# A pairwise interaction kernel with gathered embeddings: longer flights of gathers, seven product slots, a 2 KB descriptor scratch and another order of the work

## What is computed

```python
e = jnp.stack([tbl_0[ids[:, 0]], ..., tbl_31[ids[:, 31]]], axis=1)   # (2048, 32, 64)
row_idx, col_idx = np.triu_indices(32, k=1)
z = jnp.einsum('bpe,fpe,bpf->bp', e[:, row_idx, :], kernel, e[:, col_idx, :])
h = jnp.concatenate([z, dense_ctx], axis=1)
h = jnp.maximum(h @ W_top1 + b_top1, 0.0)
h = jnp.maximum(h @ W_top2 + b_top2, 0.0)
y = h @ W_top3
```

## Time and profile before

| what | us |
|---|---|
| median of 3 runs | 840.17 |
| lowest, highest | 839.22, 840.34 |
| the profiled execution | 839.88 |
| its span, first to last instruction | 838.1 |
| PE, DVE, ACT, POOL busy in the span | 753.0, 651.5, 644.2, 484.0 |
| mean granted clock of PE | 0.976 of full speed |

### The profile page before, as it was taken

How to read it: one execution, slowest core, us unless ns; L and a number is a source line. 1 busy time by engine, 2 the same in 40 slices (tenths; PEclk the granted TensorE clock), 3 DMA queues, 4 the chain that set the end, 5 groups by cost and what they waited for, 6 DMA issues and landing times.

```text
span 838.1 us, 16496 instructions
## 1 busy us (share of the span) xinstructions
PE 753.0 (90%) x4672; PEld 305.5 (36%) x4672; DVE 651.5 (78%) x601; ACT 644.2 (77%) x5196; POOL 484.0 (58%) x518
## 2 busy tenths in 40 slices
PE   0498969889898999999947998999999999999998
PEld 0244545355533333333312233333343333333333
DVE  0388969779677878999946896898978999789950
ACT  0279988967649728899953698799786999999952
POOL 6776776767676776666666766666766666000000
PEclk9999999999999999999979998999999999999999
DMA  9611111211212121111212121121122112000100
GB/s 335 204 40 38 40 38 25 52 25 38 51 27 50 26 51 25 32 42 23 51 24 50 25 48 24 24 50 25 25 50 41 31 24 51 1 2 1 27 1 0
DMA packets 34644, 36.40 MB, mean 43 GB/s; under 512 B 18676, under 2 KB 20980, under 8 KB 34424
## 3 DMA queue, kind: packets, MB, share of 16 engines
q0 software_dynamic: 16384, 16.81, 11.0%
q1 hardware_dynamic: 18168, 18.53, 7.6%
HBM read 26.91 MB, written 0.01 MB: 32 GB/s over the span
## 4 chain that ended last, share of the span: by engine, by line
PE 48%; POOL 31%; issue 11%; DMA 9%; DVE 0%; DVEq 0%; ACT 0%; POOLq 0%
POOL rows L407 21%; PE y_ps L507 15%; PE y_ps L529 11%; POOL kept_rows L407 10%; PE sum_ps L543 9%; DMA rows<-tbl_dram,idx 7%; PE layer_ps L559 3%; DMA kept_rows<-tbl_dram,idx 2%; PE layer_ps L562 2%; PE y_ps L465 1%; PE y_ps L576 1%; PE y_ps L522 1%; PE y_ps L585 1%; PE y_ps L510 1%; PE y_ps L580 0%
## 5 line engine op out<-in xcount | busy, mean ns | idle before, releaser
L669 ACT ACTIVATE batch_products<-batch_products 128x64 f32<-128x64 f32 x2576 | 615.4, 242 | 105.5 <-DVE batch_products L763 105.3
L669 ACT ACTIVATION_READ_ACCUMULATOR batch_products<-batch_products 128x1 f32 x2576 | 486.4, 189 | 0.0
L407 POOL DMA_INDIRECT rows<-tbl_dram,idx x384 | 362.4, 944 | 168.9 <-issue 102.1
L752 DVE TENSOR_TENSOR products<-y_ps,xt 128x1024 f32<-128x1024 f32 (+1 forms) x224 | 255.5, 1197 | 44.2 <-PE y_ps L508 38.5
L763 DVE TENSOR_TENSOR batch_products<-y_ps,kept_rows 128x1024 f32<-128x1024 f32 x192 | 225.1, 1216 | 24.7 <-PE y_ps L531 16.7
L507 PE MATMUL y_ps<-xt,kernel_sb 64*128 64x512 f32 (+1 forms) x448 | 207.8, 598 | 0.4 <-DVE products L752 0.3
L508 PE MATMUL y_ps<-xt,kernel_sb 64*128 64x512 f32 (+1 forms) x448 | 207.8, 598 | 0.0
L529 PE MATMUL y_ps<-kernel_sb,xt 64*128 64x512 f32 x384 | 196.1, 639 | 4.8 <-DVE products L744 2.5
L531 PE MATMUL y_ps<-kernel_sb,xt 64*128 64x512 f32 x384 | 196.1, 639 | 0.0
L543 PE MATMUL sum_ps<-products,selector 128*32 128x512 f32 (+1 forms) x1520 | 155.9, 523 | 4.2 <-ACT z_sb L639 1.7
L407 POOL DMA_INDIRECT kept_rows<-tbl_dram,idx x128 | 120.9, 945 | 57.3 <-issue 35.5
(11 more groups left out here) (54 smaller groups left out, 408.7 us busy)
## 6 DMA issues: line engine op xcount, KB each, us to landing
kernel_sb<-pair_kernel_dram SPq DMA_DIRECT2D x15, 512.0 KB, 11.2
rows<-tbl_dram,idx POOLq DMA_INDIRECT x384, 2.5
special<-xt SPq DMA_DIRECT2D x48, 128.0 KB
kept_rows<-tbl_dram,idx POOLq DMA_INDIRECT x128, 2.5
special<-xt SPq DMA_DIRECT2D x32, 64.0 KB
w_sb<-w_dram SPq DMA_DIRECT2D x1, 1024.0 KB
w_sb<-w_dram SPq DMA_DIRECT2D x1, 512.0 KB
kernel_sb<-pair_kernel_dram SPq DMA_DIRECT2D x1, 256.0 KB, 3.1
```

The source lines that it names most:

```text
L407: pool.indirect_dma_start(rows_of(g, q, t)[:, h, :], None, tables[j], bass.IndirectOffsetOnAxis(ap=idx[:, n, j:j + 1], axis=0)).then_inc(l ...
L669: last = nc.scalar.activation(product, product, ACT.Copy, accum_out=batch_sums(unit)[:, column:column + 1])
L752: nc.vector.tensor_tensor(into[:, :, 0:size], y[:, :, 0:size], by, ALU.mult).then_inc(unit_done, 1)
```

## The change

Flights begin at each second pair in all whole chunks, as they did in chunk 1 alone. The ring of products has seven slots instead of four, 12 KB more of each partition. The scratch for descriptors is 2048 bytes, 14 KB less. The strings of the order are new: 101 bursts in place of 82, with up to nine product units in one, most turns behind the batches (the sixth digit) instead of ahead of them (the second). No instruction's form changes; nine more turn steps are made of pairs that stood two in a step.

```diff
-PRODUCT_RING = 4
+PRODUCT_RING = 7
@@
-    "050201 300000 120400 310000 210300 420200 500100 220500 400100 300203 400100 400200 460501 300200",
-    "420300 320200 420200 400100 420300 600000 300400 420100 320100 300100 500000 323610T 424300 412300",
-    "412200 511000 400100 310010 412300 411300 402400 411100 411400 411300 401401 401200 400200 401300",
-    "420100 421300 420100 400200 420100 401500 411301 401301T 411400 412100 412400 402300 411400 400110",
-    "411400 410010 411201 401500 402320 410010 423300 402000 411300 411300 401400T 411300 401200 412300",
-    "411300 411430 402300 401410 413300 401300 401400 411100 402400 400000 502000 300000T",
+    "000006 000402 400301 200000 000101 400301 200001 000200 000001 700100 000001 600301 900000 100002 210601",
+    "400000 000003 400403 700502 100101 700200 200102 000202 400500 500200 600302 800001 101000T 002000 003001",
+    "001001 000300 400121 003351 400521 200200 001101 504301 600401 300301 600201 400400 400101 300400 500200",
+    "600101 000001 400302 700000 000100 100200 600202 402001 000300 100100 002101T 400120 300001 100100 000221",
+    "402511 003000 500301 401000 000001 713400 300100 200201 400200 200301 002021 400300 701200 503501 512201",
+    "400200 000001 200201 400400 000001 500301 703502T 501401 100100 500001 100500 104101 714500 614301 700000",
+    "010200 404500 101010 500300 000001 602600 600100 000100 200200 600120 600000T",
@@ def opens_flight(field):
-    if half(g):
-        return h == 0 and q % 4 == 0
-    if chunk(g) == 1:
-        return h == 0 and q % 2 == 0
-    return h == 0
+    return h == 0 and q % (4 if half(g) else 2) == 0
@@ def kernel(**inputs):
-    nc = bacc.Bacc("TRN2", target_bir_lowering=False, num_devices=1)
+    nc = bacc.Bacc("TRN2", target_bir_lowering=False, num_devices=1, dynamic_dma_scratch_size=2048)
```

## The result

| what | before | after |
|---|---|---|
| median, us | 839.86 | 817.84 |
| lowest, highest, us | 839.22, 840.34 | 816.36, 820.01 |
| profiled execution, its span, us | 839.88, 838.1 | 820.01, 818.2 |

After takes 0.974 of before, 95% interval 0.9717 to 0.9763: 22 us less. The forecast was 792.0, so 48 us less, with a range of 785 to 812. The time is 26 us above the forecast and 6 above the range. The direction is right, the size less than half of what I said.

The account below looks back on a forecast made before the run. Gathers and the PE work behind them bind: pair (4, 7) landing 602.3, PE 158.0 and last tower 25 make 785.3; the longest chain, 788 over DVE, plus 2 for long rounds gives span 790, time 792 us, range 785 to 812.

Parts of the forecast that it names:

- What binds before: Before: gathers up to pair (3, 15), landing at 528.4, then PE's work behind it; sum 835.9 against a span of 838.1.
- Flights of sixteen: POOL, segments 3 and 4: 16 of 46 openings go, each worth 1.5 us; flights alone bring 12 us.
- Order, changes of form: PE: 63 fewer changes and fewer units directly after turns make 12.6 us; order alone brings 30 with more work ahead.
- Seven product slots: DVE's product ring: slots cost nothing, allow longer rounds; PE's waits in these taken as 2 us, ends 0 and 17.
- Both: Flights and order together: pair (4, 7) binds, landing at 602.3, with 158.0 of PE work and 25 behind it: 785.3.
- Scratch 0: POOL's gathers: the 2 KB descriptor scratch costs 0 us, as only two or three gathers are in flight.
- ScalarE no bound: ScalarE's batch column sums: the chain of landing, ACT's work and PE's rest gives 787.6 at (4, 13), under 788.
- clock 0: PE's clock after idle waits: waits shrink and slow stretches are made good, so nothing is added.
- A: PE in long rounds: ring of three too short, all surplus falls on the path, time 807; chance 0.13.
- B: POOL: descriptor room forces one more wait in each flight, time 831, or 840 if each 14 gathers; chance 0.11.
- C: POOL, L407: the small scratch makes gathers themselves slower, 914 and more; chance 0.04.
- D: POOL: fewer openings gain nothing because the next wait grows; only the order counts, time 812; chance 0.02.

Follow-up runs that it names:

- the halved kernel: After with DVE multiplying only one of the two PSUM banks of each duo and quad: 796.55 us, beside before at 842.81.

## Why the prediction was wrong, point by point

- *What binds before*: right. Flights alone took 13.3 us off, 12 forecast, from a chain through pair (3, 15), which is transposed at 518.9 there. Halving DVE's products did not help before.
- *Flights of sixteen*: openings (30, of 1.8 us), gather time and landing are as said; the last gather is 6 us late, 4.8 of them by a slot wait. "POOL runs freely" was wrong by that.
- *Order, changes of form*: 63 fewer, 12.6 us. That PE's own work fell by this is my count and not a run; the span fell by 19.9, so 7.3 are left for all else.
- *Seven product slots*: **the step that failed.** "The cover for PE in a round is the ring of three PSUM buffers: ... so after some nine units without a sum or layer ... PE waits", and "DVE's surplus passes two units (2.4 us)". I counted buffers, two of them full ahead of DVE, as 2.4 us of cover. Measured, they cover 0.23 us, since the rest of the loop is used by the way from PE to DVE (1.07) and back (1.27). Waits begin at the fifth unit, not after nine. I took 2 us, with an end of 17. In its place the starts behind two full units show 24.2 us in after and 5.3 in before, and halving the multiplication takes 21 us or more off the time. No run gave PE a fourth buffer, so the ring is shown by the distances and by the shorter multiplication, not by a longer ring; nor did one give the old order seven slots.
- *Both*: (4, 7) didn't bind in after, but did in the halved kernel, landing 6 us later than forecast. With PE at DVE's pace the gathers were early, and the 20 us for flights in the new order shrank to 3.
- *Scratch 0, ScalarE no bound, clock 0*: right, for the scratch and ScalarE by a run each (ScalarE to within 4 us), for the clock by 1.00 in the stretches of after. In the halved kernel, where PE waits for gathers again, the clock fell once and cost some 1.7 us.
- *Rivals.* A had the mechanism and the sign to look for (PE before L507 or L529 on DVE), and after shows it. Its price of 807 used the same wrong cover and is 11 us too low. The chance of 0.13 came from where the long rounds stand, an argument that gathers would hide them; they didn't, because late gathers were what the order took away. B, C and D are out: POOL has no new idle time inside a flight, gathers take 0.944 us, and the openings still cost 1.8.

Some of the 109.5 us isn't DVE's. Two waits for ScalarE appear or grow in after: PE at the first sum of a bank (3.0 us, before 1.7), and PE at a layer step, for ScalarE to free the one bank that consecutive groups share (2.4 us, before none).

```profile
144.50 2.79 PE L540 MATMUL sum_ps<-products,selector 128*32 128x256 f32 x24 [2.39 <-ACT z_sb L636]
...
235.19 1.99 PE L556 MATMUL layer_ps<-z_sb,w_sb 128*128 128x512 f32 x4 [0.78 <-ACT h_sb L649]
```

No run took them away, so what they cost the whole is not shown.

## What to carry to other kernels

Price a ring of buffers by its loop, not by the number of buffers: from the producer's start to the consumer's, and from the consumer's to the producer's next use, both read from one timeline, against the number of buffers times the producer's time. When that slack is small, a consumer slower by a third (1.13 us against 0.86) shows from the second turn of the ring on, even though it is only 87 to 93% busy over the stretch, and longer rounds can cost more than they save in changes of form. And two remedies for the same wait need not add up: here earlier gathers and more work ahead of them brought 13 and 20 us alone and 22 together. Ask for each what is late next.

## What was unexpected of the hardware

- A full-looking PE: 79.98 of 80 us busy, while units in long rounds start 1.13 us apart in place of 0.86, one after another. Only distances between starts show it.
- A scratch of 2048 bytes in place of 16384 costs nothing: 0.9998 of the time in the old order (0.9989 to 1.0008), and in after, with flights of 16 gathers of 128 rows throughout, a gather takes 0.944 us as before and none waits for a place inside a flight.
- Chips on which the same kernel takes 1208 to 1249 us in place of 840, with DVE's and POOL's instructions unchanged, DVE idle up to 36.9 us for no releaser in the trace, and on which the parts even rank otherwise (flights alone 1.03, on the others 0.984). A comparison is worth something only beside before on the same chip, and with that chip's time looked at first.
